# A two-block transformer chain on one core: a static loop replaced by an unrolled program with a second, transposed set of scores

## The chip, the cores and the metric

One Trainium2 chip, one NeuronCore of it. The metric is the device time of one execution in microseconds (us). All data are float32.

## The reference

Sixteen independent batches of 128 positions by 256 channels, a condition vector and a context of 128 positions each. First block: self-attention, top-16 cross-attention, gated MLP, each behind a layer norm whose scale and shift come from the condition, each added with a gate. Second block: plain cross-attention to the modulated, normalised context. All attentions have 16 heads of 16 channels over 128 queries and 128 keys.

```python
m = silu(mod) @ w_ada + b_ada            # nine rows of 256: shift, scale, gate x 3
h = _ln(x) * (1 + sc_msa) + sh_msa
x = x + self_attn(h) * g_msa             # softmax over all 128 keys
h = _ln(x) * (1 + sc_mca) + sh_mca
q = h @ w_q + b_q; k, v = split(ctx @ w_kv + b_kv)
scores = einsum('bqhd,bkhd->bhqk', q, k) / sqrt(D)
top_s, top_i = top_k(scores, 16)         # softmax over the 16 greatest keys of each query and head
x = x + (einsum('bhqk,bhqkd->bqhd', softmax(top_s), v[top_i]) @ w_co + b_co) * g_mca
x = x + swiglu(_ln(x) * (1 + sc_mlp) + sh_mlp) * g_mlp        # hidden size 1024
# second block
xq, xkv = ada_ln(x), ada_ln(ctx)
return x + (softmax(q @ k.T / sqrt(D)) @ v) @ Wp + bp
```

## The kernel before, in words

The program has an opening and a loop of four iterations (three in a hardware loop, the last written out), each on four batches ("slots"). Within an iteration the work is a list of 48 units: 3 kinds of attention (SELF, CROSS, LAST) x 4 slots x 4 units of four heads, in this order of kinds. Each unit is one step t; `PLAN` (L64 to L89) says at which step the dense parts (norms, projections, MLP) of each slot are issued, `AHEAD` those that belong to the next iteration. Every engine walks the same steps in its own order (`body`, five times), and semaphores tie them.

One unit of attention on the engines:

- TensorE multiplies the queries (128 channels at a time) with block-diagonal keys `k_blocks` of four heads into one PSUM bank, 128 queries on partitions x 4 heads x 128 keys (L939). Three banks take turns.
- VectorE takes each head's maximum (L777). For CROSS it runs `top_k` (L633): MAX8 (L640), MATCH_REPLACE8 with a very negative number (L646), MAX8 (L652), MATCH_REPLACE8 (L657), four heads each, on PSUM first and then on the tile `left`.
- ScalarE computes the exponentials with minus the maximum as bias and sums each row on the way (L573): four activations, each with a read of the accumulator.
- SELF and LAST: VectorE inverts the row sums (L783) and GpSimd multiplies (L484). CROSS: GpSimd makes a 0/1 mask of `left` (L492) and multiplies (L496); the division comes on the value sums (L766, L768).
- TensorE transposes the four 128x128 weights (L926), ScalarE copies them out of PSUM (L567), and TensorE sums the values, 32 array columns per pair of heads (L956; for CROSS also with ones for the divisor).
- VectorE takes the result to `o_t` (L770), TensorE projects it (L884), VectorE applies the gate and adds the residual (L725, L730).

Dense parts: VectorE computes statistics (L677, L680), GpSimd the inverse root (L435, L438), VectorE the norm (L685), TensorE transposes it (L852; the context raw and normed, L858, L860), ScalarE applies scale and shift (L533). Projections are L866 (query), L875 and L878 (key, value), L884, MLP up L897, down L904; VectorE adds query, key and value biases (L691, L703, L709). SyncE spreads the keys of eight heads into `k_blocks` with eight DMAs (`place_k`, L337, L343). The opening's modulation of all batches is L822; the gate rows go to DRAM and come back broadcast to 128 partitions, and the loop starts after that.

Of the kernel before, what the change touches and what calls it, by code (L numbers as in the profile page):

```python
# [10 lines left out]
P = 128  # L20
# [5 lines left out]
HC = P // D  # L26
HID = 1024
HB = HID // P
SLOTS = 4
ITERS = B // SLOTS  # L30
QH = 4
PHASES = 3 * SLOTS
UNITS = PHASES * (H // QH)
RING = 6
FILLS = PHASES // RING
GONE = -(2.0 ** 127)

SELF, CROSS, LAST, MLP, CTX = range(5)
LNS = {SELF: 1e-6, CROSS: 1e-6, MLP: 1e-6, LAST: 1e-5, CTX: 1e-5}
NMOD = 4 * len(LNS)  # L40
NBIAS = 18 + 4 + 4 + 4 + 2 + 2 + 2 + 2 + 16

SCORE_AHEAD, TURN_LAG, SUM_LAG, O_LAG = 1, 3, 4, 5
SCORE_BANKS, TURN_BANKS, DENSE_BANKS = 3, 2, 2

EARLY, ON_TIME, LATE = range(3)


def dve_order(part):
    if part[0] in ("norm", "glu"):
        return EARLY
    return LATE if part[0] == "kv" or part[:2] == ("out", SELF) or part[0] == "q" and part[1] != LAST else ON_TIME
# [6 lines left out]
PLAN, AHEAD = {}, {}  # L64


def _put(step, *part):
    if step < 0:
        AHEAD.setdefault(step + UNITS, []).append(part)
    else:  # L70
        PLAN.setdefault(step, []).append(part)


for _s in range(SLOTS):
    _first = 4 * _s
    for _step, *_part in (
            (-8, "stats", SELF), (-6, "norm", SELF), (-6, "turn", SELF), (-5, "kv", SELF), (-5, "q", SELF),
            (3, "skip", SELF), (8, "out", SELF), (9, "stats", CROSS), (10, "skip", CROSS), (11, "norm", CROSS),
            (11, "turn", CROSS), (12, "q", CROSS), (5, "stats", CTX),
            (7, "norm", CTX), (7, "turn_ctx", CTX), (10, "kv", CROSS), (18, "kv", LAST)):  # L80
        _put(_first + _step, *_part, _s)
    _first += 4 * SLOTS
    for _step, *_part in (
            (8, "out", CROSS), (8, "stats", MLP), (9, "norm", MLP), (9, "turn", MLP), (9, "skip", MLP),
            (10, "up", 0), (11, "glu", 0), (11, "up", 1), (12, "glu", 1), (12, "out", MLP),
            (12, "stats", LAST), (13, "norm", LAST), (13, "turn", LAST), (13, "skip", LAST),
            (14, "q", LAST), (24, "out", LAST)):
        _put(_first + _step, *_part, _s)
STEPS = range(-SCORE_AHEAD, max(max(PLAN), UNITS + O_LAG - 1) + 1)  # L89

DENSE_USES = {"q": 1, "kv": 1, "turn": 1, "turn_ctx": 1, "out": 1, "up": 2}
NTH, COUNT = {}, {}
for _plan in (AHEAD, PLAN):
    for _t in sorted(_plan):
        for _part in _plan[_t]:
            _sort = {"turn_ctx": "turn"}.get(_part[0], _part[0])
            NTH[_part] = COUNT.get(_sort, 0)
            COUNT[_sort] = NTH[_part] + 1  # L100
for _t in sorted(AHEAD):
    for _part in AHEAD[_t]:
        for _u in PLAN:
            for _other in PLAN[_u]:
                assert _u <= _t or _other[0].split("_")[0] != _part[0].split("_")[0], (_part, _other)


DENSE, DENSE_FIRST, N_DENSE, N_FIRST = {}, {}, 0, 0
for _t in sorted(AHEAD):
    for _part in AHEAD[_t]:  # L110
        DENSE_FIRST[_part] = N_FIRST
        N_FIRST += DENSE_USES.get(_part[0], 0)
for _t in STEPS:
    for _part in PLAN.get(_t, []) + AHEAD.get(_t, []):
        DENSE[_part] = N_FIRST + N_DENSE
        N_DENSE += DENSE_USES.get(_part[0], 0)

DENSE_LAST, _n = {}, N_FIRST
for _t in STEPS:
    for _part in PLAN.get(_t, []):  # L120
        DENSE_LAST[_part] = _n
        _n += DENSE_USES.get(_part[0], 0)
assert N_DENSE % DENSE_BANKS == 0
GATE = {SELF: 0, CROSS: 1, MLP: 2}
N_OUT = COUNT["out"]


WEIGHTS = {("out", SELF): ("so",), ("kv", CROSS): ("kv",), ("q", CROSS): ("q",), ("out", CROSS): ("co",),
           ("up", 0): ("m1",), ("out", MLP): ("m2",), ("kv", LAST): ("lkv",), ("q", LAST): ("lq",),
           ("out", LAST): ("lp",)}  # L130
SCALED = {("q", CROSS): 2, ("q", LAST): 3}
KV_ORDER = [part[1:] for part in sorted((q for q in NTH if q[0] == "kv"), key=NTH.get)]
QUERY_BIAS = {SELF: 26, CROSS: 30, LAST: 34}
KEY_BIAS = {SELF: 28, CROSS: 32, LAST: 36}


def block_kernel(nc, a, out):

    with ExitStack() as ctx:
# [3 lines left out]
        def bank(name):  # L143
            return ctx.enter_context(nc.psum_tensor(name, [P, 512], F32))

        def sem(name):
            return ctx.enter_context(nc.semaphore(name))

# [11 lines left out]
        w_query = {SELF: w_qkv[:, :, 0:C], CROSS: w_q[:], LAST: l_q[:]}  # L160
        w_key = {SELF: w_qkv[:, :, C:2 * C], CROSS: w_kv[:, :, 0:C], LAST: l_kv[:, :, 0:C]}
        w_value = {SELF: w_qkv[:, :, 2 * C:3 * C], CROSS: w_kv[:, :, C:2 * C], LAST: l_kv[:, :, C:2 * C]}
        w_out = {SELF: w_so, CROSS: w_co, LAST: l_p}

        b_value = sb("b_value", P, 3, C)
        b_out = sb("b_out", P, 4, C)
        bias_rows = sb("bias_rows", NBIAS, P)
        bias_cols = sb("bias_cols", P, NBIAS)
        mod_bias = sb("mod_bias", P, NMOD)

        silu_t = sb("silu_t", P, CK, B)
        mod_all = sb("mod_all", P, B, NMOD)
        mod_now = sb("mod_now", P, SLOTS, NMOD)

        ident = sb("ident", P, P)
        minus_half = sb("minus_half", P, 1)
        one_cols = sb("one_cols", P, 2, 32)

        x_in = sb("x_in", P, SLOTS, C)
        ctx_in = sb("ctx_in", P, SLOTS, C)  # L180
        gates = sb("gates", P, SLOTS, 3 * C)
        x_mid = sb("x_mid", P, SLOTS, C)
        x_skip = sb("x_skip", P, SLOTS, C)
        gated = sb("gated", P, C)
        x_norm = sb("x_norm", P, 3, C)
        ln_stats = sb("ln_stats", P, 4, 6)
        ln_mv = sb("ln_mv", P, 4, 2)
        ln_var = sb("ln_var", P, 4, 1)
        ln_rstd = sb("ln_rstd", P, 4, 1)
        h_t = sb("h_t", P, SLOTS, CK, P)  # L190
        ctx_t = sb("ctx_t", P, 1, CK, P)
        ctx_norm_t = sb("ctx_norm_t", P, 3, CK, P)
        q_t = sb("q_t", P, RING, CK, P)
        k_t = sb("k_t", P, 3, CK, P)

        k_blocks = sb("k_blocks", P, RING, CK, HC, P)

        v_pad = sb("v_pad", P, RING, H // 2, 2, 32)
        neg_max = sb("neg_max", P, 4, QH)
        row_sum = sb("row_sum", P, 4, QH)  # L200
        probs = sb("probs", P, 4, QH, P)
        left = sb("left", P, 4, QH, P)
        top8 = sb("top8", P, 2, QH, 8)
        probs_t = sb("probs_t", P, 3, QH, P)
        inv_sum = sb("inv_sum", P, CK, P)
        o_t = sb("o_t", P, CK, P)
        lin_a = sb("lin_a", P, 2, 4, P)
        tanh_a = sb("tanh_a", P, 2, 4, P)
        half_b = sb("half_b", P, 2, 4, P)
        glu = sb("glu", P, HB, P)  # L210
        gate_rows = glu[0:B].rearrange("p j t -> p (j t)")[:, 0:3 * C]
        gates_dram = nc.dram_tensor("gates_dram", (B, 3 * C), F32).ap()


        FIRST = 2
        arena = k_blocks[:, FIRST:].rearrange("p r c h t -> p (r c h t)")
        NADA = 9 * C
        w_ada = arena[:, 0:CK * NADA].rearrange("p (c n) -> p c n", c=CK)
        ss_q = arena[:, CK * NADA:CK * (NADA + 2 * C)].rearrange("p (c n) -> p c n", c=CK)
        ss_kv = arena[:, CK * (NADA + 2 * C):CK * (NADA + 4 * C)].rearrange("p (c n) -> p c n", c=CK)  # L220

        spare = arena[0:B, CK * (NADA + 4 * C):]
        gate_bias = spare[:, 0:3 * C]
        cond, cond_tanh, cond_silu = (spare[:, n * C:(n + 1) * C] for n in (3, 4, 5))

        score_bank = [bank(f"score_bank{n}") for n in range(SCORE_BANKS)]
        turn_bank = [bank(f"turn_bank{n}") for n in range(TURN_BANKS)]
        o_bank = bank("o_bank")
        dense_bank = [bank(f"dense_bank{n}") for n in range(DENSE_BANKS)]
        o_view = o_bank[:].rearrange("p (c k t) -> p c k t", c=CK, k=2)  # L230


        cond_loaded = sem("cond_loaded")
        ada_loaded = [sem(f"ada_loaded{k}") for k in range(3)]
        ss_loaded = sem("ss_loaded")
        rows_loaded = sem("rows_loaded")
        b_value_loaded = sem("b_value_loaded")
        b_out_loaded = sem("b_out_loaded")
# [60 lines left out]

        def phase_of(kind, s):  # L300
            return SLOTS * kind + s


        @block.sync
        def _(sp):
# [709 lines left out]
```

## Time and profile before

| what | value |
|---|---|
| median of 3 runs | 1002.02 us (998.5 to 1002.84) |
| span of the profiled execution, first to last instruction | 996.2 us |
| mean granted TensorE clock | 0.916 of full |
| TensorE (PE) busy | 792.8 us, 80% |
| TensorE weight loads (PEld) busy | 587.8 us, 59% |
| VectorE (DVE) busy | 667.5 us, 67% |
| ScalarE (ACT) busy | 513.2 us, 52% |
| GpSimd (POOL) busy | 502.1 us, 50% |
| share of the span's closing chain | PE 40%, DVE 36%, issue 10%, ACT 5% |
| HBM traffic | 21.20 MB read, 2.15 MB written |

Busy counts an engine's instructions without waits. The chain is followed back from the last instruction, each step to what released it. A float32 matmul is two records, a transpose one, and some records may be missing. "Clock" is the share of full speed that TensorE was granted. In the rows PE is TensorE, PEld its weight loads, L a line of the kernel, and "x" a number of instructions; after a second bar stands the idle time before a group and what ended it.

### The profile page before, as it was taken

The numbers are of one execution on the slowest core, as the hardware profiler recorded it, in microseconds if no ns is written. First come the engines' busy times: TensorE is split into PE (matmuls) and PEld (weight loads), VectorE is DVE, ScalarE is ACT, GpSimd is POOL, SyncE is SP. The second block draws the span as 40 slices with busy tenths as digits, with TensorE's granted clock in tenths as the row PEclk, the third lists the DMA queues.
The fourth block names the chain that finished last, engine by engine and source line by source line (L and its number), as shares of the span: only waits on it lengthen the run. The fifth ranks groups of instructions, "written<-read, shape, count | busy, mean of one in ns | idle before, by whom it ended". The sixth has DMA issues, their size and how long they took to land.

```text
span 996.2 us, 21054 instructions
## 1 busy us (share of the span) xinstructions
PE 792.8 (80%) x5919; PEld 587.8 (59%) x5919; DVE 667.5 (67%) x2576; ACT 513.2 (52%) x2068; POOL 502.1 (50%) x576
## 2 busy tenths in 40 slices
PE   4869677788879865898887967778898886589987
PEld 3546446676646543676664645657665664377764
DVE  2348888855546888875445688886545689888543
ACT  1258334455558543355565844435565864335556
POOL 3246656544336655554443665455433665556344
PEclk9789789799999976989999988799999997898999
DMA  7351000000000100000000100000000000000000
GB/s 268 110 178 33 17 25 15 18 23 17 27 26 20 31 22 17 22 10 28 24 15 23 29 17 24 16 22 22 17 23 27 12 12 12 12 7 7 1 7 17
DMA packets 33860, 31.15 MB, mean 31 GB/s; under 512 B 7613, under 2 KB 29363, under 8 KB 33475
## 3 DMA queue, kind: packets, MB, share of 16 engines
q1 hardware_dynamic: 33731, 29.66, 10.0%
q8 instruction: 53, 0.87, 0.4%
q14 instruction: 76, 0.62, 0.2%
HBM read 21.20 MB, written 2.15 MB: 23 GB/s over the span
## 4 chain that ended last, share of the span: by engine, by line
PE 40%; DVE 36%; issue 10%; ACT 5%; POOL 3%; SPq 2%; DMA 2%; DVEq 1%; POOLq 0%; ACTq 0%
PE dense_bank L897 10%; PE score_bank L939 7%; DVE left L646 6%; DVE left L657 6%; DVE top L640 5%; DVE top L652 4%; PE dense_bank L904 4%; PE turn_bank L926 4%; PE dense_bank L866 4%; ACT probs L573 3%; PE dense_bank L875 3%; PE o_bank L956 3%; DVE ln_stats L677 2%; PE dense_bank L878 2%; PE dense_bank L884 2%
## 5 line engine op out<-in xcount | busy, mean ns | idle before, releaser
L573 ACT ACTIVATE probs<-score_bank,neg_max 128x128 f32<-128x128 f32 x768 | 272.2, 372 | 254.4 <-DVEq L650 168.7
L939 PE MATMUL score_bank<-k_blocks,q_t 128*128 128x512 f32 x384 | 216.1, 651 | 10.8 <-issue 6.3
L484 POOL TENSOR_TENSOR probs<-probs,row_sum 128x512 f32<-128x512 f32 x128 | 133.1, 1047 | 67.0 <-DVE row_sum L783 66.7
L573 ACT ACTIVATION_READ_ACCUMULATOR probs<-score_bank,neg_max 128x1 f32 x768 | 161.4, 210 | 0.0
L567 ACT COPY probs_t<-turn_bank 128x512 f32<-128x512 f32 x192 | 113.2, 590 | 89.1 <-PE turn_bank L926 80.2
L897 PE MATMUL dense_bank<-h_t,w_m 128*128 128x128 f32 x1024 | 134.4, 293 | 12.2 <-DVEq L694 11.5
L897 PEld LDWEIGHTS dense_bank<-h_t,w_m 128*128 128x128 f32 x1024 | 128.5, 207 | 21.1 <-ACT h_t L533 10.8
L435 POOL TENSOR_SCALAR ln_var<-ln_mv 128x1 f32<-128x1 f32 x80 | 15.2, 190 | 228.3 <-DVE ln_mv L680 226.6
L492 POOL TENSOR_SCALAR left<-left 128x512 f32<-128x512 f32 x64 | 95.5, 1492 | 68.7 <-DVE left L657 68.0
L852 PE MATMUL dense_bank<-ident,x_norm 128*128 128x128 f32 x128 | 32.2, 340 | 107.4 <-DVEq L712 54.0
L777 DVE TENSOR_REDUCE neg_max<-score_bank 128x4 f32<-128x512 f32 x128 | 87.2, 682 | 25.3 <-PE score_bank L939 22.0
L926 PE MATMUL turn_bank<-ident,probs 128*128 128x128 f32 x512 | 80.6, 281 | 22.1 <-POOL probs L484 22.0
L852 PEld LDWEIGHTS dense_bank<-ident,x_norm 128*128 128x128 f32 x128 | 15.7, 161 | 126.7 <-issue 67.7
L496 POOL TENSOR_TENSOR left<-left,probs 128x512 f32<-128x512 f32 x64 | 81.8, 1279 | 9.2 <-POOL left L492 7.9
L926 PEld LDWEIGHTS turn_bank<-ident,probs 128*128 128x128 f32 x512 | 60.7, 143 | 36.7 <-POOL probs L484 29.3
L464 POOL TENSOR_TENSOR glu<-tanh_a,half_b 128x512 f32<-128x512 f32 x32 | 40.7, 1272 | 73.0 <-ACT half_b L549 73.0
L939 PEld LDWEIGHTS score_bank<-k_blocks,q_t 128*128 128x128 f32 x384 | 64.3, 207 | 22.1 <-issue 16.0
L956 PEld LDWEIGHTS o_bank<-probs_t,v_pad 128*32 128x32 f32 x1536 | 36.1, 109 | 69.0 <-issue 52.5
L533 ACT ACTIVATE h_t<-dense_bank,mod_now 128x128 f32<-128x128 f32 x128 | 52.2, 468 | 46.5 <-PE dense_bank L852 44.3
L646 DVE MATCH_REPLACE8 left<-top,score_bank 128x128 f32<-128x128 f32 x256 | 70.0, 283 | 0.0
L657 DVE MATCH_REPLACE8 left<-top,left 128x128 f32<-128x128 f32 x256 | 67.8, 276 | 0.3
L956 PE MATMUL o_bank<-probs_t,v_pad 128*32 128x128 f32 x1536 | 61.8, 279 | 3.0 <-ACT probs_t L567 3.0
(110 smaller groups left out, 1424.8 us busy)
## 6 DMA issues: line engine op xcount, KB each, us to landing
k_blocks<-k_t SPq DMA_DIRECT2D x384, 16.0 KB, 1.8
gates<-gates_dram SPq DMA_DIRECT2D x16, 384.0 KB, 3.4
k_blocks<-in_L_xcond_w_ada SPq DMA_DIRECT2D x3, 768.0 KB, 9.3
x_in<-in_x SPq DMA_DIRECT2D x16, 128.0 KB, 2.2
ctx_in<-in_ctx SPq DMA_DIRECT2D x16, 128.0 KB, 2.7
w_m<-in_L_xcond_w_m SPq DMA_DIRECT2D x1, 2048.0 KB, 11.9
out_y<-x_mid SPq DMA_DIRECT2D x16, 128.0 KB, 1.7
w_m<-in_L_xcond_w_m SPq DMA_DIRECT2D x1, 1024.0 KB, 13.7
```

The costliest lines, as they stand in the source:

```text
L484: nc.gpsimd.tensor_tensor(probs[:, u % 4], probs[:, u % 4], row_sum[:, u % 4].unsqueeze(2).broadcast_to([P, QH, P]), ALU.mult).then_inc(we ...
L492: nc.gpsimd.tensor_scalar(left[:, t % 4], left[:, t % 4], GONE, None, ALU.is_equal).then_inc(mask_done, 1)
L496: nc.gpsimd.tensor_tensor(left[:, t % 4], left[:, t % 4], probs[:, t % 4], ALU.mult).then_inc(weights_ready, 1)
L567: nc.scalar.copy(probs_t[:, u % 3].rearrange("p h t -> p (h t)"), turn_bank[u % TURN_BANKS][:]).then_inc(probs_t_ready, 1)
L573: e = nc.scalar.activation(probs[:, t % 4, h], score_bank[t % SCORE_BANKS][:, P * h:P * h + P], ACT.Exp, bias=neg_max[:, t % 4, h:h + 1], ...
L646: e = nc.vector.match_replace(l[:, h], top8[:, 0, h], bank_u[:, P * h:P * h + P], GONE)
L657: e = nc.vector.match_replace(l[:, h], top8[:, 1, h], l[:, h], GONE)
L777: nc.vector.tensor_reduce(neg_max[:, t % 4], score_bank[t % SCORE_BANKS][:].rearrange("p (h t) -> p h t", t=P), AX.X, ALU.max, negate=True ...
L897: e = nc.tensor.matmul(d[:, P * j:P * j + P], w_m1[:, c, at:at + P], h_t[:, s, c], start=(c == 0), stop=(c == CK - 1))
L926: e = nc.tensor.transpose(turn_bank[u % TURN_BANKS][:, P * h:P * h + P], src[:, u % 4, h], ident[:])
L939: nc.tensor.matmul(score_bank[u % SCORE_BANKS][:], q_t[:, r, c], k_blocks[:, r, c, blk:blk + 4].rearrange("p h t -> p (h t)"), start=True, ...
L956: e = nc.tensor.matmul(o_view[32 * g:32 * g + 32, c, what], w, probs_t[:, (u - 1 + g // 2) % 3, 2 * (g % 2) + odd], start=(odd == 0), stop ...
```

## The change

Loop, slots and units go. A table `DUE` names each part of the work and gives for each of the 16 batches a due time; each engine's program is the list of its parts in the order of due times, fully unrolled (`program_of`). `Homes` assigns buffers in that order; the wait before a refill is for the parts that read the buffer last. Parts of many batches and of all kinds of attention are mixed. The work itself changes in these points:

- **Two sets of scores.** `scores` (queries on partitions) serves the maxima and the top-k alone. `tscores` computes the scores again with keys on partitions, so the exponentials need no transpose. Both use one set of four PSUM banks `quad[0..3]`, filled by matmuls that contract 32 rows (two heads), one row group of the array per bank.
- **Maximum and mask in PSUM.** Minus the maxima (`neg_max`) are transposed (`turnmax`, `rowmax`), and a 32-row matmul with the selector `sel` adds them. For C the mask (`second`'s tile scaled so that kept keys are 128 more than removed ones, times `minus_ident`) is added by full matmuls.
- **Exponentials** are one activation of 128x512 per bank, without bias or row sums. `sum` multiplies them with values and a column of ones, 17 columns a head; the division (`inv`, `divide`) is on the sums, which are then transposed (`turnsum`).
- **Engines.** ScalarE copies the C scores out (`copy`), so the top-k reads SBUF, and writes out queries, keys, values, `lin_a` and projections. GpSimd does norms, residuals and divisions. VectorE keeps statistics, maxima, top-k, silu, inverses and the last addition.
- **Inputs.** The host passes biases and condition laid out, and the context transposed too (`ctx_t`), so the raw context is not transposed on the core. Value biases are folded into rows added with the residual (`bias_proj`, `const_proj`). `x` keeps all batches in SBUF; gate rows still pass through DRAM, but nothing waits for them until `skip` and `resid`.

```diff
-PLAN, AHEAD = {}, {}
...
+DUE = {
...
+    "scores S": (1776, 2213, 3267, 3627, 4932, 5330, 7156, 7660, 9984, 12814, 13198, 17158, 19634, 22436, 26393, 28835,),
...
+    "tscores S": (2575, 2931, 3993, 4596, 6082, 6442, 8026, 9618, 11006, 13645, 15184, 18307, 20619, 24861, 27216, 30619,),
...
+    "scores C": (5699, 6778, 9178, 11342, 12471, 15867, 17668, 20041, 22946, 25431, 28082, 30988, 33006, 34975, 37770, 39808,),
...
+    "tscores C": (8628, 10486, 11875, 14634, 16596, 18670, 21538, 23979, 25840, 29719, 31946, 33975, 36145, 38818, 40575, 42389,),
...
+    "scores L": (21061, 23538, 26836, 28409, 31328, 33333, 35754, 38262, 40151, 41960, 43763, 44130, 46287, 46661, 47830, 48842,),
...
+    "tscores L": (22058, 24519, 27626, 29232, 32651, 34634, 37374, 39472, 41167, 43071, 44628, 45149, 47018, 47494, 48321, 49262,),
...
+def program_of(engine):
+
+    parts = [(t, name, i) for name, times in DUE.items() if name.split()[0] in ENGINE[engine]
+             for i, t in enumerate(times)]
+    return [(name, i) for _, name, i in sorted(parts)]
...
+        quad_homes = Homes(1, {
+            **{f"scores {k}": tuple(f"max {k} {g}" for g in range(G)) for k in "SL"},
+            "scores C": tuple(f"copy {g}" for g in range(G)),
+            **{f"tscores {k}": tuple(f"exp {k} {g}" for g in range(G)) for k in "SCL"}})
...
+                elif verb == "mask":
+
+                    u = left[:, left_homes.at[f"first {k}", i]]
+                    pool.wait_ge(*after(f"second {k}", i))
+                    nc.gpsimd.tensor_scalar(u, u, 2.0 ** -120, 128.0, ALU.mult, ALU.add).then_inc(done[verb], 1)
...
+                    nc.gpsimd.tensor_tensor(divided[:, d], sums[:, s, :, 0:D],
+                                            sums[:, s, :, D + 1:D + 2].broadcast_to([P, H, D]),
+                                            ALU.mult).then_inc(done[verb], 1)
...
+                    nc.scalar.activation(exps[:, exp_homes.at[f"tscores {k}", i], int(g)].rearrange("p j t -> p (j t)"),
+                                         quad[int(g)][:], ACT.Exp).then_inc(done[verb], 1)
...
+                    for h in range(4):
+                        nc.vector.max(top[:, h], src[:, h]).then_inc(top_step, 1)
+                    for h in range(4):
+                        dve.wait_ge(top_step, n_top + h + 1)
+                        e = nc.vector.match_replace(dst[:, h], top[:, h], src[:, h], GONE)
...
+                elif verb == "scores":
...
+                    for c in range(CK):
+                        for r in range(G):
+                            at = slice(32 * r, 32 * r + 32)
+                            if c == 0 and free:
+                                pe.wait_ge(*free[r])
+                            e = nc.tensor.matmul(quad[r][:, C * c:C * c + C], q[at, c],
+                                                 kb[at, c].rearrange("p a t -> p (a t)"), start=True, stop=True)
...
+                elif verb == "tscores":
...
+                    for j in range(4):
+                        for r in range(G):
+                            at = slice(32 * r, 32 * r + 32)
+                            if j == 0 and free:
+                                pe.wait_ge(*free[r])
+                            nc.tensor.matmul(quad[r][:, P * j:P * j + P], kb[at, j // 2, j % 2], q[at, j // 2],
+                                             start=True, stop=False)
+                        for r in range(G):
+                            at = slice(32 * r, 32 * r + 32)
+                            e = nc.tensor.matmul(quad[r][:, P * j:P * j + P], sel[at, j], m[at],
+                                                 start=False, stop=(k != "C"))
+                        if k == "C":
+                            for r in range(G):
+                                if j == 0:
+                                    pe.wait_ge(*after(f"mask {r}", i))
+                                    pe.wait_ge(ones_ready, 4)
+                                e = nc.tensor.matmul(quad[r][:, P * j:P * j + P],
+                                                     left[:, left_homes.at[f"first {r}", i], j], minus_ident[:],
+                                                     start=False, stop=True)
+                    e.then_inc(done[verb], 1)
+                elif verb == "sum":
...
+                    for r in range(G):
+                        pe.wait_ge(*after(f"exp {k} {r}", i))
+                        for j in range(4):
+                            h = 8 * (j // 2) + 2 * r + j % 2
+                            e = nc.tensor.matmul(d[:, (D + 1) * h:(D + 1) * (h + 1)], exps[:, src, r, j],
+                                                 v_aug[:, v_homes.at[value, i], h], start=True, stop=True)
+                    e.then_inc(done[verb], 1)
```

## Rows read from the trace of the kernel before

**Rows 1.** Clock and span of the core, and the engine totals of the page.

```profile
core 0: 996.2 us, clock 0.916
...
PE 792.8 (80%) x5919; PEld 587.8 (59%) x5919; DVE 667.5 (67%) x2576; ACT 513.2 (52%) x2068; POOL 502.1 (50%) x576
```

**Rows 2.** Stretches of 10 us: busy us, mean granted clock (PEclk), DMA share, GB/s.

```profile
80.00:90.00 10.00, 10.00 (x84) 6.97 (x83) 7.15 (x20) 9.00 (x41) 7.72 (x11) 1.00 0.16 41
110.00:120.00 10.00, 3.31 (x28) 1.79 (x27) 8.91 (x47) 4.05 (x19) 7.91 (x8) 0.84 0.01 2
```

**Rows 3.** Waits, longest in total first: us in total, times, longest.

```profile
PE dense_bank L852 <- DVEq L712: 54.0, 8, 8.5
...
PE dense_bank L852 <- DVE x_norm L685: 53.4, 35, 5.0
```

**Rows 4.** Chain of waits in order of time: start us, us, what.

```profile
50.66 7.70 DMA gates_dram<-glu
```

**Rows 5.** Timeline of TensorE: start us, us from first start to last end.

```profile
504.20 0.59 PE L939 MATMUL score_bank<-k_blocks,q_t 128*128 128x512 f32 x1
504.73 0.65 PE L956 MATMUL o_bank<-probs_t,v_pad 128*32 128x128 f32 x16
505.30 1.16 PE L875 MATMUL dense_bank<-h_t,w_qkv 128*128 128x128 f32 x8
506.30 1.03 PE L878 MATMUL dense_bank<-w_qkv,h_t 128*128 128x256 f32 x4
507.16 1.05 PE L866 MATMUL dense_bank<-h_t,w_qkv 128*128 128x128 f32 x8
508.05 0.60 PE L926 MATMUL turn_bank<-ident,probs 128*128 128x128 f32 x4
508.49 1.02 PE L939 MATMUL score_bank<-k_blocks,q_t 128*128 128x512 f32 x2
509.35 0.38 PE L884 MATMUL dense_bank<-l_p,o_t 128*128 128x256 f32 x1
```

**Rows 6.** Groups of TensorE, shapes apart: busy us, mean ns of one.

```profile
L897 PE MATMUL dense_bank<-h_t,w_m 128*128 128x128 f32 x1024 | 134.4, 293 | 12.2 <-DVEq L694 11.5 <-DVEq L712 0.6
...
L904 PE MATMUL dense_bank<-w_m,glu 128*128 128x256 f32 x256 | 57.9, 379 | 0.0
...
L866 PE MATMUL dense_bank<-h_t,w_q 128*128 128x128 f32 x128 | 18.3, 290 | 0.0
...
L878 PE MATMUL dense_bank<-l_kv,ctx_norm_t 128*128 128x256 f32 x64 | 17.8, 405 | 0.0
...
L956 PE MATMUL o_bank<-probs_t,v_pad 128*32 128x128 f32 x1536 | 61.8, 279 | 3.0 <-ACT probs_t L567 3.0
```

**Rows 7.** The modulation (L822) alone, window 35.60 to 37.80 us.

```profile
35.60:37.80 2.20, 2.20 (x22) 2.20 (x22) 1.00 0.12 27
```

**Rows 8.** Groups of VectorE: top-k and maxima.

```profile
L777 DVE TENSOR_REDUCE neg_max<-score_bank 128x4 f32<-128x512 f32 x128 | 87.2, 682 | 25.3 <-PE score_bank L939 22.0 <-DVE q_t L691 1.3 <-issue 1.2
...
L646 DVE MATCH_REPLACE8 left<-top,score_bank 128x128 f32<-128x128 f32 x256 | 70.0, 283 | 0.0
...
L640 DVE MAX8 top<-score_bank 128x8 f32<-128x128 f32 x256 | 56.4, 281 | 1.6 <-DVE q_t L691 1.2
```

**Rows 9.** Groups of ScalarE and GpSimd in attention.

```profile
L573 ACT ACTIVATE probs<-score_bank,neg_max 128x128 f32<-128x128 f32 x768 | 272.2, 372 | 254.4 <-DVEq L650 168.7 <-DVE neg_max L777 85.4
...
L573 ACT ACTIVATION_READ_ACCUMULATOR probs<-score_bank,neg_max 128x1 f32 x768 | 161.4, 210 | 0.0
...
L484 POOL TENSOR_TENSOR probs<-probs,row_sum 128x512 f32<-128x512 f32 x128 | 133.1, 1047 | 67.0 <-DVE row_sum L783 66.7
L567 ACT COPY probs_t<-turn_bank 128x512 f32<-128x512 f32 x192 | 113.2, 590 | 89.1 <-PE turn_bank L926 80.2
L492 POOL TENSOR_SCALAR left<-left 128x512 f32<-128x512 f32 x64 | 95.5, 1492 | 68.7 <-DVE left L657 68.0
```

**Rows 10.** DMA issues of the key blocks: KB each, median us to landing.

```profile
k_blocks<-k_t SPq DMA_DIRECT2D x384, 16.0 KB, 1.8
```

More of the change, by code:

```diff
@@ L54, in dve_order @@
[L54 to L57, printed above, removed]
-PLAN, AHEAD = {}, {}
[L67 to L105, printed above, removed]
@@ L108 @@
[L108 to L133, printed above, removed]
@@ new lines @@
+ENGINE = {
+    "sync": ("cond", "bias", "ada", "w", "rowpack", "bp", "ldx", "ldk", "ldt", "place", "rows", "rows_out", "store"),
+    "gpsimd": ("rstd", "norm", "skip", "mask", "negmax", "divide", "resid", "glu", "skip_rows"),
+    "scalar": ("mod", "query_out", "value_out", "keys_out", "copy", "rowmax", "exp", "sum_out", "turnsum_out",
+               "proj_out", "tanh", "lin_b", "lin_a"),
+    "vector": ("stats", "max", "first", "second", "inv", "silu", "last", "silu_cond", "bias_fix", "mod_add",
+               "gate_add", "const_add"),
+    "tensor": ("turn", "query", "value", "keys", "scores", "turnmax", "tscores", "sum", "turnsum", "proj", "up",
+               "modulate", "gates", "bias_proj", "const_proj"),
+}
@@ L141, in sb, with attentions @@
             return ctx.enter_context(nc.sbuf_tensor(name, list(shape), F32))
-        def bank(name):
-            return ctx.enter_context(nc.psum_tensor(name, [P, 512], F32))
         def sem(name):
             return ctx.enter_context(nc.semaphore(name))
+        def attentions(fills, ends):
+            return {f"{fills} {k}": tuple(f"{e} {k}" for e in ends) for k in "SCL"}
+        dense_homes = Homes(4, {
+            **{f"turn {k}": (f"mod {k}",) for k in KINDS},
+            **{f"query {k}": (f"query_out {k}",) for k in "SCL"}, "value S": ("value_out S",),
+            **{f"keys {k}": (f"keys_out {k}",) for k in "CL"},
+            **attentions("turnmax", ["rowmax"]), **attentions("sum", ["sum_out"]),
+            **attentions("turnsum", ["turnsum_out"]),
+            **{f"proj {k}": (f"proj_out {k}",) for k in "SCM"}, "proj L": ("last L",),
+            **{f"up {w} {h}": (f"lin_{w} {h}",) for w in "ab" for h in range(2)},
+            **{f"modulate {k}": (f"mod_add {k}",) for k in "SCML"},
+            "gates 0": ("gate_add 0",), "gates 1": ("gate_add 1",), "bias_proj": ("gate_add 2",),
+            "const_proj": ("const_add",)})
@@ new lines, in block_kernel @@
+        hk_homes = Homes(3, {"mod K": ("keys L",)})
+        ctx_homes = Homes(3, {"ldk": ("norm K",)})
+        ctx_t_homes = Homes(3, {"ldt": ("keys C",)})
+        rows_homes = {k: Homes(2, {f"rows {k}": (f"resid {k}",)}) for k in "SCM"}
+        q_homes = Homes(4, attentions("query_out", ["tscores"]))
+        kt_homes = Homes(3, {"query_out S": ("place S",), "keys_out C": ("place C",), "keys_out L": ("place L",)})
+        block_homes = Homes(8, attentions("place", ["tscores"]))
+        v_homes = Homes(9, {"value_out S": ("sum S",), "keys_out C": ("sum C",), "keys_out L": ("sum L",)})
@@ new lines, in block_kernel @@
+        neg_homes = Homes(3, {"scores S": ("turnmax S",), "scores L": ("turnmax L",), "negmax": ("turnmax C",)})
+        row_homes = Homes(2, attentions("rowmax", ["tscores"]))
+        exp_homes = Homes(2, attentions("tscores", ["sum"]))
+        copy_homes = Homes(5, {f"copy {g}": (f"first {g}",) for g in range(G)})
+        left_homes = Homes(6, {f"first {g}": ("tscores C",) for g in range(G)})
+        sum_homes = Homes(2, attentions("sum_out", ["divide"]))
+        div_homes = Homes(2, attentions("divide", ["turnsum"]))
@@ L150, in block_kernel @@
+        sum_t_homes = Homes(2, attentions("turnsum_out", ["proj"]))
+        proj_homes = Homes(2, {f"proj_out {k}": (f"resid {k}",) for k in "SCM"})
+        lin_a_homes = Homes(2, {f"lin_a {h}": (f"silu {h}",) for h in range(2)})
+        lin_b_homes = Homes(2, {f"lin_b {h}": (f"glu {h}",) for h in range(2)})
+        tanh_homes = Homes(4, {f"tanh {h}": ("proj M",) for h in range(2)})
         w_qkv = sb("w_qkv", P, CK, 3 * C)
@@ L199, in block_kernel @@
[L199 to L211, printed above, removed]
@@ L223, in block_kernel @@
[L223 to L234, printed above, removed]
@@ L500, in _ @@
[L500 to L510 removed]
+                                    base=0, pattern=[[-1, P]], channel_multiplier=1).then_inc(ident_ready, 1)
@@ L900, in dense_part @@
-                if name == "out" and kind == MLP:
-                    for j in range(HB):
-                        if j % 4 == 0:
-                            pe.wait_ge(glu_done, i * COUNT["glu"] + NTH["glu", j // 4, s] + 1)
-                        e = nc.tensor.matmul(d[:, 0:C], glu[:, j], w_m2[:, j],
-                                             start=(j == 0), stop=(j == HB - 1))
-                    e.then_inc(dense_ready, 1)
-            def dense_parts(i, t, more):
-                for part in PLAN.get(t, ()):
-                    dense_part(part, i, i * N_DENSE, i * (N_DENSE // DENSE_BANKS),
-                               (DENSE if more else DENSE_LAST)[part])
-                for part in AHEAD.get(t, ()) if more else ():
-                    dense_part(part, i + 1, i * N_DENSE, i * (N_DENSE // DENSE_BANKS), DENSE[part])
```

1394 lines of the change are left out of this document (705 added, 689 removed), and 132 rows, old and new, of the table DUE.

## The prediction

> **What bounds the kernel now.** I read the engine totals first. TensorE is the busiest engine, 792.8 us of a span of 996.2 us, at a mean granted clock of 0.916 [rows 1]. Then the stretches: they alternate. In a self-attention stretch TensorE is busy for all 10 us at full clock; in a cross-attention stretch VectorE is busy 8.91 of 10 us with the top-k and TensorE 3.31 [rows 2]. So the loop runs one kind of attention at a time, and the two busiest engines take turns. The waits say the same: TensorE's two longest waits (54.0 and 53.4 us) end with VectorE [rows 3]. In the chain of waits the loop also stands behind the gates' trip to DRAM and back, 7.70 us from 50.66 us on for the way out alone, before its first step [rows 4].
>
> How much of the 792.8 us is work at full clock? A busy stretch gives the pace, from start to next start [rows 5]. 8 records with 128 moving columns take 0.89 us (507.16 to 508.05), 0.111 each; a float32 matmul is two records. 4 with 256 columns take 0.86 (506.30 to 507.16), 0.215 each. 4 transposes take 0.44, 0.11 each. Two with 512 take 0.86, 0.43 each. The value sums (L956) use 32 array columns each, four groups at once: 16 records in 0.57 us. If each round of four lasts 0.11 like a transpose, that is 0.44 and 0.13 for leaving this form; entering it makes the last 512-column record last 0.53 in place of 0.43. So four tiles run side by side, 0.0275 us a record, and one excursion into a tiled form costs 0.23 us.
>
> Times the counts [rows 6]: 1024 + 6 x 128 = 1792 records of 128 columns, 199 us; 256 + 6 x 64 = 640 of 256 columns, 138; 512 + 256 + 192 transposes, 106; 384 score records, 165; 2048 tiled ones in 128 bursts of 0.57, 73; the opening's modulation 12. Sum 693 us. The span is 303 us longer: gaps and slow clock.
>
> **The change, TensorE.** All else is compared with this queue, since it becomes the fullest.
>
> Kept: 1792 and 640 records, 199 + 138 = 337 us. Removed: the transposes of probabilities and contexts, the full-height scores, the 32-column sums. Added or replaced, for 16 batches x 3 attentions = 48 phases:
> - Transposes: 5 norms x 2 x 16, turnsum 2 x 48, turnmax 48 = 304, 33 us.
> - Sums: 16 matmuls a phase, weights 128x128 (exps), 17 moving columns; 1536 records. The nearest row is the modulation (L822), the same weights and 16 columns: 22 records touch a window of 2.20 us, and by the rate inside it one starts about each 0.11 us [rows 7]. It saves nothing over 128 columns. 1536 x 0.111 = 170 us.
> - The mask added in PSUM: 16 full matmuls a cross phase, 512 records, 57 us.
> - scores: 8 matmuls of 32 rows, 256 columns: 16 records a phase. tscores: 32 matmuls of 32 rows, 128 columns: 64 records. The trace has no 32-row tile. Lower bound: four row groups side by side as the four column groups are, 192 rounds x 0.215 + 768 rounds x 0.11 = 41 + 84 = 125 us. Upper bound: one after another, 768 x 0.215 + 3072 x 0.111 = 506. I take the lower: the L956 rows are the same array cut the other way, and each of the four banks quad0 to quad3 has its own row group, which permits it.
> - Excursions into the 32-row form: one per scores (48), one per tscores S and L (32), four per tscores C, where the mask matmuls stand between (64): 144 x 0.23 = 33 us.
> - Opening (modulate, gates, bias and constant projections): 80 records of 0.111 and 24 of 0.215, 14 us.
>
> Sum: 337 + 33 + 170 + 57 + 125 + 33 + 14 = 769 us, **76 more than now**. The change gains nothing on TensorE; all of the gain has to come from the 303 us.
>
> The Trainium skill ("TensorE: Matmul & The Clock Gate", section "The mechanism" of Part 3 with the table under it) says loads and matmuls of different row groups overlap, and gives 3.07x for four tiles of 32 rows and 512 columns. Estimated from that page, the 125 us would be 506 / 3.07 = 165, and the time 40 us more. No row here shows 32-row tiles.
>
> **The change, the others.** They must stay under TensorE.
> - VectorE keeps the top-k: MAX8 56.4 + 55.9, MATCH_REPLACE8 70.0 + 67.8, value loads about 42 = 292 us, and 87 for the maxima [rows 8]. With statistics (49), silu (25), inverses of 16 numbers (9, at 0.18 each) and the last additions (7) about 470, from 667.5. The norms, residuals, query, key and value outputs leave it.
> - ScalarE: 768 exponentials and accumulator reads (272.2 + 161.4) become 192 of 128x512 without sums; priced as the copy of that size, 0.59 each [rows 9], 113 us. The copies of probs_t (113.2) go, 64 score copies come (38). Added: outputs of query, keys, value, lin_a, sums and projections. With an estimated 0.29 for a 128x128 output and 0.38 for 128x256, about 450 us in all, from 513.2.
> - GpSimd loses the normalisation of probabilities (133.1) [rows 9] and the mask's multiplication; it gains norms, residuals and divisions: 325 us, or up to 425 if all its 128x512 and 128x256 tensor_scalars run at the 1.49 us per 512 of L492 [rows 9]; it had 502.1.
> - SyncE still issues 8 key DMAs a phase, 384, landing in 1.8 us [rows 10]. About 5 us a phase is 242 us of its queue, and behind a waiting one stand the row loads and stores. The due times leave these early; I cost them at nothing. If that cover goes, a scores step starts up to 5 us late.
> - Four banks serve both score sets. An S or L phase holds them for 0.9 (scores) + 2.7 (four maxima) + about 1 (turnmax, rowmax) + 1.8 (tscores) + 2.4 (exps), 8.8 us; a C phase about 12. Per batch 30, in all 480 us: under TensorE. What hides the 4 to 5 us between a scores and its tscores is other TensorE work: in the written order 7 us or more for every S, 36 or more for every C, 6 or more for every L but the last (1).
>
> I use the due times for their order alone. Cut into 25 equal pieces, every piece but the first holds 17 to 40 us of TensorE's work by the paces above, and only the last but one under 23; VectorE's 470 us are 19 a piece. So after the opening TensorE should hardly stand.
>
> **The sum.** 769 of work; a clock as in the dense stretches, mean 0.98, adds 16; the opening 20 idle (loads, modulation, first statistics; now it is 46 and the gates' trip); the last batch's L phase 12 (its scores-to-tscores wait 3, then exps, sum, division, turn, projection, store 9); 2% of waits in between 16. That is 833 of span. The profiled execution has 996.2 against a median of 1002.0, 5.8 outside: **840 us**. Own range of this case 800 to 910: the page's rate for tiles, and idle from half to twice of what I took.
>
> **Rivals.**
> - A. 32-row tiles don't run side by side, because each loads 128 weight columns where an L956 tile loads 32. For: in the L822 rows the load alone sets the pace. Against: the four loads of L956 overlap. Price: 506 instead of 125, +381 at full height; if only the weight loads queue, 3840 x 0.111 = 426, +301. The time is 1140. It decides from (1002 - 840) / 3840 = 0.042 more, 0.075 us a record. The side slower than before; chance 0.17. The skill's page ("LDWEIGHTS (loading the stationary operand)") says that 32 rows take as long to load as 128; by it alone this rival would hold.
> - B. TensorE is in order, and the order was planned for other durations than the chip's: it waits at tscores for a maximum that stands in VectorE's queue behind a top-k part of 2.3 us, or on a late key DMA, or on the instruction stream, now unrolled. For: now it stands 303 us. Against: the cover counted above. One such wait, 1.3 us at each of the 96 bank fills, is +125: 965. Chance 0.20; of it 0.13 faster, 0.03 within, 0.04 slower.
> - C. The new sums are cheaper than L822, as 17 columns could let loads alone run faster: if 0.09 a record, 1536 x 0.02 = -31 us and 810. Inside the first case.
>
> **How the numbers follow.** The first case 0.63, B 0.20, A 0.17. Half a per cent is what a measurement of this kernel can tell. Faster 0.63 + 0.13 = 0.76, same 0.03, slower 0.21. Range 800 to 1040: A and a little below 800 are left out.
>
> **What would show it.** Right: TensorE busy over 90% of a span near 835 with clock 0.97 or more; sum records 0.11 apart; scores and tscores in rounds of four that start within a few hundredths of a us and repeat each 0.11 or 0.215; VectorE near 470, ScalarE 450; no alternation between stretches. A: tscores S takes 7 us instead of 1.8, TensorE over 95% and a span over 1100. B: TensorE's waits list tscores, scores or sum with over 100 us. Wrong in another way: VectorE or GpSimd busier than TensorE.

## The result and the profile after

The changed kernel takes 982.68 us (median of 4 runs, 974.34 to 990.84) against 1001.88 before. Two of the four runs took 975 us, and two 990 at a slightly lower clock; the ratio, 0.9731 with a 95% interval of 0.9702 to 0.976, compares the two faster ones with the kernel before. Faster, as forecast, but by 2.7% where 840 us had promised 16%. The profiled execution has a span of 973.4 us.

The core's clock and the engine totals of the changed kernel, to be read beside [rows 1]:

```profile
core 0: 973.4 us, clock 0.860
...
PE 935.8 (96%) x8728; PEld 840.0 (86%) x8728; DVE 397.1 (41%) x1938; ACT 410.3 (42%) x1139; POOL 356.5 (37%) x652
```

TensorE is busy for 96% of the span, and every other engine is under half (PEld, the weight loads, is TensorE's own). VectorE and ScalarE are lower than I had summed (470 and 450). But the mean clock fell from 0.916 to 0.860. The page's 40 slices show the same: TensorE full throughout, clock not.

```profile
PE   7999997999899999999999999999999999999996
...
PEclk9968878778887997979789989887999799797965
```

The chain that ended last is nearly all TensorE, and the new sums (L1026) are its largest line:

```profile
PE 94%; ACT 3%; issue 1%; DMA 0%; DVE 0%; ACTq 0%; POOL 0%; POOLq 0%; SPq 0%; DVEq 0%
PE dense L1026 23%; PE dense L1054 13%; PE quad L1014 7%; PE dense L944 7%; PE quad L978 7%; PE quad L1003 7%; PE dense L1040 6%; PE dense L1046 5%; PE quad L1007 5%; PE dense L962 3%; PE dense L965 3%; PE dense L935 2%; PE dense L1033 2%; PE dense L951 1%; ACT exps L701 1%
```

TensorE's waits, which were 54.0 and 53.4 us at the top [rows 3], are now led by one in the opening:

```profile
PE dense L905 <- DVE silu_t L757: 5.7, 1, 5.7
PE dense L1026 <- ACT exps L701: 3.6, 2, 2.3
PE dense L1033 <- ACT q_t L654: 3.0, 1, 3.0
```

The groups of TensorE's new work (busy us, mean ns of one):

```profile
L1026 PE MATMUL dense<-v_aug,exps 128*128 128x17 f32 x1536 | 232.1, 301 | 7.4 <-ACT exps L701 3.6 <-ACT q_t L654 2.5 <-ACT sums_t L715 1.1
...
L1003 PE MATMUL quad<-q_t,k_blocks 32*128 32x128 f32 x1536 | 92.3, 308 | 2.6 <-ACT exps L701 2.0 <-issue 0.5
L1007 PE MATMUL quad<-max_rows,sel 32*128 32x128 f32 x1536 | 82.1, 282 | 0.0
...
L1014 PE MATMUL quad<-minus_ident,arena 128*128 128x128 f32 x512 | 75.0, 290 | 0.0
...
L978 PE MATMUL quad<-k_blocks,q_t 32*128 32x256 f32 x768 | 69.6, 482 | 1.5 <-ACT exps L701 1.3 <-ACT q_t L654 0.2
```

**Were the 32-row tiles as quick as taken?** The timeline of TensorE at full clock answers (start us, us from first start to last end):

```profile
515.05 1.15 PE L978 MATMUL quad<-k_blocks,q_t 32*128 32x256 f32 x16
516.13 0.64 PE L988 MATMUL dense<-ident,neg_max 128*128 128x128 f32 x2
...
520.63 0.50 PE L1003 MATMUL quad<-q_t,k_blocks 32*128 32x128 f32 x8
520.96 0.40 PE L1007 MATMUL quad<-max_rows,sel 32*128 32x128 f32 x8
521.18 0.40 PE L1003 MATMUL quad<-q_t,k_blocks 32*128 32x128 f32 x8
...
522.63 0.33 PE L988 MATMUL dense<-ident,neg_max 128*128 128x128 f32 x1
```

Eight records of 128 columns go in 0.22 us (520.96 to 521.18), so four at once in 0.11: the pace of the column tiles. The tscores of an S phase take 2.00 us in all (520.63 to 522.63), where the prediction has 1.8 and one excursion of 0.23; its scores take 1.08 (515.05 to 516.13), where it has 0.86 + 0.23. Rival A is out.

**Where did the clock go?** The timeline around one fall, and the stretches just before and after it (busy us of PE, PEld, DVE, ACT, POOL, then the granted clock):

```profile
358.76 3.62 PE L1040 MATMUL dense<-w_m,arena 128*128 128x256 f32 x16
362.21 10.32 PE L1026 MATMUL dense<-v_aug,exps 128*128 128x17 f32 x64
372.37 0.67 PE L935 MATMUL dense<-ident,x_norm 128*128 128x128 f32 x2
```

```profile
362.40:365.80 3.40, 3.40 (x32) 3.40 (x33) 2.00 (x14) 1.88 (x4) 2.74 (x6) 1.00 0.12 27
365.90:369.30 3.40, 3.40 (x18) 3.40 (x17) 0.00 (x0) 0.39 (x1) 0.50 (x1) 0.50 0.29 80
372.60:376.00 3.40, 3.40 (x24) 2.54 (x23) 0.72 (x3) 2.16 (x6) 2.10 (x5) 0.50 0.00 0
376.20:379.60 3.40, 3.26 (x31) 3.04 (x27) 3.23 (x9) 1.40 (x6) 0.56 (x1) 1.00 0.16 39
```

In the rows the granted clock has two levels, 1.00 (2.4 GHz) and 0.50 (1.2 GHz). TensorE never stands in the first three stretches. It runs two phases of sums in a row, 64 records of 17 moving columns; 32 of them touch the first stretch at 2.4 GHz, 18 the second at 1.2 GHz. The clock is back only after other matmuls. Of the 29 falls in this trace, 26 begin within or right behind a burst of L1026, one behind the opening's modulation with 16 moving columns (L905), and two after TensorE had stood. So the profile suggests a culprit; the experiments have to show it. The mean of 0.860 means 2 x 0.14 x 973.4 = 273 us at the lower level. Span times clock, 0.860 x 973.4 = 837 us, estimates the span at full clock; it takes everything at the lower level to be twice as slow. The sum records are only 1.9 times as slow there (0.112 and about 0.21 us apart), so 837 is on the low side.

### The profile page after: what moved, and what is told of

Its sections match the earlier page's. It is cut to its first block, busy times and chain, and to the rows that moved or that the text cites. A ratio compares the mean times of both kernels' runs of the same rounds, so it can differ in the third digit from the quotient of the medians.

```text
span 973.4 us, 23755 instructions
## 1 busy us (share of the span) xinstructions
PE 935.8 (96%) x8728; PEld 840.0 (86%) x8728; DVE 397.1 (41%) x1938; ACT 410.3 (42%) x1139; POOL 356.5 (37%) x652
## 4 chain that ended last, share of the span: by engine, by line
PE 94%; ACT 3%; issue 1%; DMA 0%; DVE 0%; ACTq 0%; POOL 0%; POOLq 0%; SPq 0%; DVEq 0%
PE dense L1026 23%; PE dense L1054 13%; PE quad L1014 7%; PE dense L944 7%; PE quad L978 7%; PE quad L1003 7%; PE dense L1040 6%; PE dense L1046 5%; PE quad L1007 5%; PE dense L962 3%; PE dense L965 3%; PE dense L935 2%; PE dense L1033 2%; PE dense L951 1%; ACT exps L701 1%
## 5 line engine op out<-in xcount | busy, mean ns | idle before, releaser
L1026 PEld LDWEIGHTS dense<-v_aug,exps 128*128 128x128 f32 x1536 | 229.9, 240 | 16.6 <-issue 10.4
L1026 PE MATMUL dense<-v_aug,exps 128*128 128x17 f32 x1536 | 232.1, 301 | 7.4 <-ACT exps L701 3.6
L701 ACT ACTIVATE exps<-quad 128x512 f32<-128x512 f32 x192 | 103.2, 606 | 137.5 <-PE quad L1014 89.3
L1054 PE MATMUL dense<-h_t,w_m 128*128 128x128 f32 x1024 | 133.8, 292 | 0.7 <-ACT q_t L654 0.6
L1054 PEld LDWEIGHTS dense<-h_t,w_m 128*128 128x128 f32 x1024 | 130.6, 208 | 2.5 <-ACT q_t L654 0.8
L818 DVE TENSOR_REDUCE neg_max<-quad 128x4 f32<-128x512 f32 x128 | 79.5, 684 | 125.3 <-PE quad L978 125.3
L621 ACT ACTIVATE arena<-dense,bias_cols 128x128 f32<-128x128 f32 x256 | 73.1, 379 | 57.2 <-PE dense L1054 57.2
L1003 PE MATMUL quad<-q_t,k_blocks 32*128 32x128 f32 x1536 | 92.3, 308 | 2.6 <-ACT exps L701 2.0
L1007 PE MATMUL quad<-max_rows,sel 32*128 32x128 f32 x1536 | 82.1, 282 | 0.0
L1014 PE MATMUL quad<-minus_ident,arena 128*128 128x128 f32 x512 | 75.0, 290 | 0.0
```

Of the source, the lines that this page charges most:

```text
L621: e = nc.scalar.activation(dst[:, j], src[:, P * j:P * j + P], ACT.Identity, scale=scale, bias=bias[:, j:j + 1])
L701: nc.scalar.activation(exps[:, exp_homes.at[f"tscores {k}", i], int(g)].rearrange("p j t -> p (j t)"), quad[int(g)][:], ACT.Exp).then_inc( ...
L818: nc.vector.tensor_reduce(neg_max[:, neg_homes.at[f"scores {k}", i], int(g), 0:4], quad[int(g)][:].rearrange("p (h t) -> p h t", t=P), AX. ...
L1003: nc.tensor.matmul(quad[r][:, P * j:P * j + P], kb[at, j // 2, j % 2], q[at, j // 2], start=True, stop=False)
L1007: e = nc.tensor.matmul(quad[r][:, P * j:P * j + P], sel[at, j], m[at], start=False, stop=(k != "C"))
L1014: e = nc.tensor.matmul(quad[r][:, P * j:P * j + P], left[:, left_homes.at[f"first {r}", i], j], minus_ident[:], start=False, stop=True)
```

## The experiments

Theory 1: the sums of 17 moving columns take the clock down. Theory 2: the 32-row tiles do, as each uses a quarter of the array. ("Ratio" below is always to the kernel before.)

**e1, e2: widen the sums.** Each matmul also writes copies of its 17 columns to the right, over places that later heads fill or that nothing reads. The result is unchanged, and so are the records and the weights; only the moving columns grow, to 119 (97 on average), or to 51 (48 on average) in e2 with 3 in place of 7.

```diff
-                            e = nc.tensor.matmul(d[:, (D + 1) * h:(D + 1) * (h + 1)], exps[:, src, r, j],
-                                                 v_aug[:, v_homes.at[value, i], h], start=True, stop=True)
+                            w = min(7, 8 - h) if h < 8 else 7
+                            e = nc.tensor.matmul(
+                                d[:, (D + 1) * h:(D + 1) * (h + w)].rearrange("p (w d) -> p w d", w=w),
+                                exps[:, src, r, j],
+                                v_aug[:, v_homes.at[value, i], h].unsqueeze(1).broadcast_to([P, w, D + 1]),
+                                start=True, stop=True)
```

> Each sum matmul moves up to 119 columns instead of 17 (97 on average, copies that later heads overwrite); same records, weights and result. Theory 1 (the 17-column sums take the clock down): sum records stay 0.112 us apart, mean granted clock back to 0.96 or more, and the span goes from 973 to about 837 / 0.97 = 863 us, as 0.86 x 973.4 = 837 us is what it needs at full clock. Theory 2 (the 32-row tiles take it down, a quarter of the array each): clock stays 0.86, span 973 or a little more.

> Up to 51 columns per sum matmul (48 on average). Theory 1: between the two, clock 0.88 to 0.97, span 865 to 955. Theory 2: unchanged, 973.

Measured: e1 866.91 us, ratio to the kernel before 0.8704 (0.8654 to 0.8755); e2 906.89, 0.9053 (0.8995 to 0.9112). Clocks and spans, e1 and then e2:

```profile
core 0: 863.9 us, clock 0.984
```

```profile
core 0: 906.5 us, clock 0.933
```

Writing up to seven times the columns makes the kernel 109.5 us faster by the profiled spans, 973.4 and 863.9. The forecast of 863 was met in part by luck, since two errors cancel: at full clock e1 needs 0.984 x 863.9 = 850 us and not 837, and the clock came back to 0.984 and not only to 0.97. Of theory 2 nothing is left: the tiles are untouched. One fall of e1's trace still comes while TensorE never stands, and it is behind the modulation, whose 16 columns the edit leaves as they are:

```profile
86.03 3.67 PE L905 MATMUL dense<-silu_t,arena 128*128 128x16 f32 x32
```

```profile
86.20:89.40 3.20, 3.20 (x31) 3.20 (x31) 1.38 (x5) 0.37 (x1) 1.74 (x5) 1.00 0.77 212
89.50:92.80 3.30, 3.30 (x22) 2.28 (x22) 0.81 (x3) 0.27 (x1) 0.17 (x1) 0.50 0.13 31
```

The other four falls come after stretches in which TensorE stood for a good part. In e1's timeline one phase of sums still takes the time that it takes at full clock with 17 columns:

```profile
356.17 3.73 PE L1027 MATMUL dense<-v_aug,exps 128*128 128x119 f32 x32
359.74 1.96 PE L1058 MATMUL dense<-h_t,w_m 128*128 128x128 f32 x16
```

From 356.17 to 359.74 is 3.57 us for 32 records, 0.112 each, as with 17 columns at full clock. So the moving columns don't set this pace; I put it down to the load of the 128 weight columns, which no run changed by itself. Up to 119 moving columns fit beside it for nothing.

**e3: a quarter of the sum matmuls.** For each bank the first head's exponentials serve all four heads; 12 of 16 sum matmuls of a phase are left out, and the other four move 68 columns. The result is a different one.

```diff
-                        for j in range(4):
-                            h = 8 * (j // 2) + 2 * r + j % 2
-                            e = nc.tensor.matmul(d[:, (D + 1) * h:(D + 1) * (h + 1)], exps[:, src, r, j],
-                                                 v_aug[:, v_homes.at[value, i], h], start=True, stop=True)
+                        cols = d[:, 0:H * (D + 1)].rearrange("p (c r w) -> p c r w", c=2, r=G)[:, :, r]
+                        v = v_aug[:, v_homes.at[value, i]].rearrange("p h d -> p (h d)").rearrange(
+                            "p (c r w) -> p c r w", c=2, r=G)[:, :, r]
+                        e = nc.tensor.matmul(cols, exps[:, src, r, 0], v, start=True, stop=True)
```

> Leaves out 12 of the 16 sum matmuls of a phase (each bank's first head's exponentials serve all its four heads, 68 columns moving). 24 records of 0.112 less in each of 48 phases, 129 us at full clock: 837 - 129 = 708. Theory 1: the clock recovers to 0.97, span about 730. Theory 2: clock 0.86 or lower, since the 32-row tiles are a larger share, span 823 or more.

Measured: 762.24 us, ratio 0.7631 (0.7593 to 0.7669).

```profile
span 758.7 us, 21451 instructions
## 1 busy us (share of the span) xinstructions
PE 704.4 (93%) x7576; PEld 615.8 (81%) x7576; DVE 396.3 (52%) x1938; ACT 404.6 (53%) x1139; POOL 357.5 (47%) x652
```

The clock is 0.976, as theory 1 says, with the tiles now a larger share of the work. The span is 29 us over the forecast: at full clock 0.976 x 758.7 = 740 instead of 708. Most of that comes from the 837 it started from. From e1's 850, which has the same records at nearly full clock, 129 less is 721; TensorE idles 54.3 us here and 39.6 in e1, which makes 736.

**e4: the scores matmuls twice.** The 32-row scores are issued a second time into the same place.

```diff
                             e = nc.tensor.matmul(quad[r][:, C * c:C * c + C], q[at, c],
                                                  kb[at, c].rearrange("p a t -> p (a t)"), start=True, stop=True)
+                        for r in range(G):
+                            at = slice(32 * r, 32 * r + 32)
+                            e = nc.tensor.matmul(quad[r][:, C * c:C * c + C], q[at, c],
+                                                 kb[at, c].rearrange("p a t -> p (a t)"), start=True, stop=True)
```

> Every 32-row scores matmul is issued twice, with the same result: 4 more rounds of 0.215 in 48 phases, 41 us at full clock. Theory 1: the low stretches stay as long as they are (275 us), span 973 + 41 = 1014 or less, mean clock 0.86 to 0.87. Theory 2: the low clock grows with the tiles, mean clock below 0.85, span over 1030. If tiles did not run four at once, +165 or more.

Measured: 1013.68 us (991.61 to 1017.26); the runs lie too far apart for a ratio, so only spans and clocks are used. The profiled run:

```profile
core 0: 1015.3 us, clock 0.869
```

At full clock 0.869 x 1015.3 = 882, 45 us more than 837, where 41 were forecast. The low level lasts 2 x 0.131 x 1015.3 = 266 us, no longer than the 273 without the extra tiles. The other three runs say the same: spans of 1013.9, 1009.4 and 989.8 us at 0.869, 0.873 and 0.897 give 881 to 888 us at full clock and 204 to 266 at the low level, where the four runs of the changed kernel have 266 to 297. More tiles don't lower the clock.

**e5: the sums as before, and a faster kernel.** The values are the weights again, 32 columns wide (two heads share the zeros between them), and the exponentials move. `turnsum` goes; the reciprocal works on 256 numbers, and its due time is put right behind `sum_out`; there are 3 buffers of `sums_t` in place of 2.

```diff
-                        for j in range(4):
-                            h = 8 * (j // 2) + 2 * r + j % 2
-                            e = nc.tensor.matmul(d[:, (D + 1) * h:(D + 1) * (h + 1)], exps[:, src, r, j],
-                                                 v_aug[:, v_homes.at[value, i], h], start=True, stop=True)
+                    for c in range(CK):
+                        for what in range(2):
+                            for odd in range(2):
+                                for r in range(G):
+                                    v = v_pad[:, v_homes.at[value, i], 4 * c + r, odd:odd + 2]
+                                    w = v.rearrange("p q d -> p (q d)") if what == 0 else one_cols[:, odd]
+                                    e = nc.tensor.matmul(d[32 * r:32 * r + 32, C * what + P * c:C * what + P * c + P], w,
+                                                         exps[:, src, r, 2 * c + odd], start=(odd == 0), stop=(odd == 1))
...
+                    nc.vector.reciprocal(inverses[:, inv_homes.at[name, i]].rearrange("p c t -> p (c t)"),
+                                         d[:, C:2 * C]).then_inc(done[verb], 1)
```

> The sums as in the kernel before: values padded to 32 columns are the weights, the exponentials move with 128 columns, four column tiles at once, with a second set of matmuls against ones for the divisor; no turnsum. Divisors are inverted by VectorE from PSUM (256 numbers, 1.75 us a phase in the kernel before), GpSimd multiplies. Theory 1: 64 records a phase in 16 rounds of 0.11 plus one excursion of 0.23 make 2.0 us in place of 3.57 + 0.22, 86 us less in 48 phases than the 850 us at full clock of the widened kernel (863.9 x 0.984), and 128 moving columns keep the clock at 0.97 or more: span about 780. If the clock fell for the 32-row tiles after all, or VectorE's reciprocals (84 us more on a 398 us engine) ended up in TensorE's way: 850 or more.

Measured: 806.64 us, ratio 0.8073 (0.8035 to 0.8111), the fastest of the kernels that leave nothing out.

```profile
span 803.8 us, 26650 instructions
## 1 busy us (share of the span) xinstructions
PE 738.5 (92%) x10168; PEld 640.9 (80%) x10168; DVE 468.7 (58%) x1938; ACT 394.7 (49%) x1091; POOL 370.0 (46%) x655
```

TensorE's busy time falls by 86 us from e1's 824.3, as priced, at a clock of 0.980. The span falls by 60, to 803.8 where about 780 was forecast: TensorE now idles 65.3 us, against 39.6 in e1, 26 more, and that is the difference. Waits that its own work had covered begin to show; which of them, I have not followed up.

**e6: less top-k.** On e1's kernel, the second pass of the top-k runs for one of four heads only, so the mask keeps 8 keys in place of 16 for the others.

```diff
-                    for h in range(4):
-                        nc.vector.max(top[:, h], dst[:, h]).then_inc(top_step, 1)
...
+                    nc.vector.max(top[:, h], dst[:, h]).then_inc(top_step, 1)
+                    dve.wait_ge(top_step, n_top + 1)
+                    nc.vector.match_replace(dst[:, h], top[:, h], dst[:, h], GONE).then_inc(done[verb], 1)
```

> On the widened kernel, leaves out the second top-k pass for three of four heads: 192 of 256 MAX8 and MATCH_REPLACE8, about 109 us of VectorE. If TensorE alone sets the time: within 0.5% of 867 us. If in-order waits for the top-k (rival B of the prediction) still cost something: faster by what they cost, up to 30 us.

Measured: 871.53 us, ratio 0.8695 (0.8642 to 0.8748), where e1 has 0.8704.

```profile
PE 831.2 (95%) x8728; PEld 745.3 (85%) x8728; DVE 319.0 (37%) x1362; ACT 409.6 (47%) x1139; POOL 359.0 (41%) x652
```

VectorE has 79 us less (109 had been priced), and nothing comes of it: the two ratios differ by 0.001, and each is known to 0.005. So in-order waits for the top-k, a part of rival B, cost at most some 7 us here.

**e7: fewer mask matmuls.** On e1's kernel, 12 of the 16 mask matmuls of a cross phase are left out (those of j = 0 to 2), and the waits for the mask stand before j = 3.

```diff
-                        if k == "C":
+                        if k == "C" and j == 3:
```

> On the widened kernel, leaves out 12 of the 16 mask matmuls of each cross phase (j = 0 to 2), and with them the switches between the 32-row form and the full form. If every TensorE record is on the path at its full-clock price: 384 records x 0.112 = 43 us plus 3 x 16 excursions x 0.23 = 11 us, 54 less, 813 us. If the excursions cost nothing, 824; if these gaps were filled from elsewhere, nearer 867.

Measured: 812.63 us, ratio 0.8127 (0.8098 to 0.8156): 54.3 less than e1, forecast 54. Run by run the spans spread: the profiled one, 801.7 us, is e7's shortest, and the other four are 810.1 to 810.8, against e1's 863.9 to 873.4. TensorE's records and its switches of form are on the path at about their full-clock price.

## Why the prediction was wrong in size and right in sign

- **TensorE becomes the bound, all others hide: right.** 96% busy; e6 takes 79 us from VectorE and moves nothing, e7 takes 54 us of TensorE's work and moves the time by 54.
- **TensorE's work at full clock, 769 us: about 41 too low.** The paces came as read: scores 1.08 and the tscores of S 2.00 us as summed, the sum records at 0.112. But e1 has 824.3 us busy, 811 with half of its 28 us at the low level taken off. Counted in e1's trace from each start to the next, the transposes take 45 us in place of 33 and the mask matmuls 68 in place of 57; the rest is spread.
- **Opening, end and waits, 20 + 12 + 16 = 48: about right.** TensorE's idle time is 39.6 us in e1 and 37.6 in the changed kernel. Work and these together were put at 817 us, and e1 needs 850 at full clock.
- **"a clock as in the dense stretches, mean 0.98, adds 16": the step that failed.** It adds 123 us: widening the moving columns alone takes 109.5 away (973.4 - 863.9), and 14 are left there (863.9 - 850). Span times clock puts it at 973.4 - 837 = 136. Of the 140 us between 833 and 973.4, this step has 107 and the work with the waits 33. I had taken the clock from the share of time in which TensorE is busy, and the dense stretches of the kernel before were filled with matmuls of 128 to 512 moving columns. The one row with the new form, the modulation with 16 columns [rows 7], I used for the pace alone. It shows 2.2 us at full clock, and its window ends 0.4 us too early: in the same burst, with TensorE never standing, the clock fell.

```profile
34.85 3.79 PE L822 MATMUL score_bank<-silu_t,k_blocks 128*128 128x16 f32 x32
```

```profile
37.80:38.20 0.40, 0.40 (x6) 0.40 (x5) 0.00 (x0) 0.00 (x0) 0.00 (x0) 1.00 0.07 17
38.20:38.60 0.40, 0.40 (x4) 0.36 (x4) 0.00 (x0) 0.00 (x0) 0.00 (x0) 0.50 0.18 41
```

  The burst of 32 such records from 24.34 us on ended in the same way. These are the only two of that trace's 27 falls before which TensorE had not stood, so the warning was there to be read.
- **"It saves nothing over 128 columns": true of the pace, and the other half was missed:** 17 columns cost the same as 119 and take the clock down with them.
- **Rival A (tiles one after another)** failed: eight records in 0.22 us. The Trainium skill's rule on the load ("TensorE: Matmul & The Clock Gate", section "LDWEIGHTS (loading the stationary operand)"), by which the time goes with the weight columns and not with the rows, agrees with the pace of the sums at full clock: with 128 weight columns it is 0.112 us at 17 moving columns and in e1's phase of up to 119. It doesn't make row groups wait for each other; that they overlap is what Part 3 of the same page of the Trainium skill says, and this trace agrees. The 3.07x that the Trainium skill gives there for four tiles, with 512 columns, was low for this kernel, which reaches 4 with 128 columns; 512 were not run here.
- **Rival B (in-order waits)** cost little; **rival C** (sums cheaper than L822) didn't come.
- **The range.** 982.68 lies inside 800 to 1040 by luck: the upper part stood there for rival B's waits, which didn't come. Of the prediction's own signs of being right, the busy share held, but "a span near 835 with clock 0.97 or more" did not.

What the change brought: by span times clock the time at full clock went from 0.916 x 996.2 = 912.5 to 837 us, 75 less, although TensorE's work grew by as much by the prediction's count. Of this, 52 went back: by the same estimate the low clock cost 84 us before (996.2 - 912.5) and 136 after. That leaves the 23 us between the two spans. The split is an estimate: measured by e1, the figures after are 850 and 123, and no run measures those before.

Open: what in a stretch of sums brings the clock down, since the traces only show where it changes. Mean clocks were taken at 17 columns, at 48 and at 97 on average; nothing in between was run.

## What to carry to other kernels

A full TensorE is no promise of a full clock: before you price a form of matmul, ask what it moves as well as how long it takes, and look up the granted clock in stretches of that same form, to their end and beyond. Where a matmul takes no longer with more moving columns, they are free, and here (up to 119) they were worth 110 us; the better cure here was to make the narrow operand the weights (e5, 60 us more). Multiply span and clock before you compare two kernels: work and clock then come apart, if only roughly (837 by the product, 850 by e1), and an error of one doesn't hide in the other.

## What the runs showed of the hardware that I had not expected

- TensorE's clock fell from 2.4 to 1.2 GHz while it never stood: 64 records of 17 moving columns in a row, 0.112 us apart before the fall (32 in 3.4 us) and about 0.21 after it (18 touch 3.4 us). The weight load slowed with it.
- The same 1536 records gave a mean clock of 0.860 with 17 moving columns, 0.933 with 48 on average, and 0.984 with 97.
- Four 32-row tiles ran in the time of one, 128 weight columns each included: eight records in 0.22 us, against eight full ones in 0.89 [rows 5].
- The clock also fell behind 16 moving columns: in the kernel before (two bursts of 32 records of L822), in the changed kernel and in e1 (L905), each time with TensorE never idle.
